# Two sequence mixers in scans of 1024 tokens instead of 512, with the other batch's PSUM banks, and a new order on every queue

## The reference

```python
# RWKV mixer, per channel, along the tokens
xk, xv, xr = mix(x, shifted)                  # and k = xk Wk', v = xv Wv', r = sigmoid(xr Wr')
p  = max(pp, u + k);  e1 = exp(pp - p);  e2 = exp(u + k - p)
out = (e1 * aa + e2 * v) / (e1 * bb + e2)
p2 = max(w + pp, k);  e1b = exp(w + pp - p2);  e2b = exp(k - p2)
aa, bb, pp = e1b * aa + e2b * v,  e1b * bb + e2b,  p2
# retention mixer: 16 heads of width 8
q, k = rope(q), rope(k)
out = einsum((q k' * 8**-0.5) * gamma**(s - t) for s >= t, v)
x += silu(x Wg') * groupnorm(out) @ Wo'
```

## Time and profile before

| | us |
|---|---|
| median of three runs (727.64 to 732.35) | 732.11 |
| the profiled execution, its own time | 732.31 |
| its span, first to last instruction | 730.4 |
| PE busy | 597.5 (82%) |
| DVE busy | 414.8 (57%) |
| POOL busy | 377.7 (52%) |
| ACT busy | 351.5 (48%) |
| mean granted TensorE clock | 0.934 |

### The profile page before, as it was taken

How to read it: one execution, slowest core, us unless ns; L and a number is a source line. 1 busy time by engine, 2 the same in 40 slices (tenths; PEclk the granted TensorE clock), 3 DMA queues, 4 the chain that set the end, 5 groups by cost and what they waited for, 6 DMA issues and landing times.

```text
span 730.4 us, 13064 instructions
## 1 busy us (share of the span) xinstructions
PE 597.5 (82%) x4172; PEld 505.0 (69%) x4172; DVE 414.8 (57%) x1166; ACT 351.5 (48%) x669; POOL 377.7 (52%) x396
## 2 busy tenths in 40 slices
PE   3489969998289888798979887999668699987892
PEld 2379968677267777788979886666434269986792
DVE  5744227797859963635056023879998896342002
ACT  2345656773158455554766554331111124665461
POOL 0467877432376337766775777124000276367762
PEclk9999989999599999998999998999799799999996
DMA  8295124001213012242231231000201012114313
GB/s 335 73 337 70 38 68 92 30 27 48 77 48 41 22 51 73 82 74 43 75 115 38 53 111 50 10 16 25 58 0 29 14 48 45 51 38 120 73 48 105
DMA packets 45120, 50.20 MB, mean 69 GB/s; under 512 B 14456, under 2 KB 36344, under 8 KB 45056
## 3 DMA queue, kind: packets, MB, share of 16 engines
q0 software_dynamic: 11776, 24.14, 14.3%
q1 hardware_dynamic: 33280, 25.23, 10.9%
HBM read 32.04 MB, written 17.29 MB: 68 GB/s over the span
## 4 chain that ended last, share of the span: by engine, by line
PE 48%; POOL 17%; DVE 14%; issue 10%; DMA 7%; ACT 3%; SPq 0%; ACTq 0%; DVEq 0%; POOLq 0%
PE bank L598 12%; POOL xs L1041 10%; PE bank L578 10%; POOL tokens_out L1051 7%; PE bank L585 6%; PE bank L677 5%; DMA xs<-tokens_in,idx_in 5%; PE bank L705 4%; PE bank L524 2%; PE bank L559 2%; DVE zT L1184 1%; PE bank L504 1%; ACT mixer L761 1%; PE bank L514 1%; DVE mixer L1321 1%
## 5 line engine op out<-in xcount | busy, mean ns | idle before, releaser
L1051 POOL DMA_INDIRECT tokens_out<-ys,idx_out x184 | 190.2, 1034 | 172.8 <-ACT ys L872 126.9
L1041 POOL DMA_INDIRECT xs<-tokens_in,idx_in x184 | 179.4, 975 | 161.2 <-DVE owner L1200 84.6
L598 PE MATMUL bank<-w,hT 128*128 x1288 | 180.9, 284 | 15.7 <-ACT ys L872 10.2
L598 PEld LDWEIGHTS bank<-w,hT 128*128 128x128 f32 x1288 | 164.1, 196 | 32.9 <-issue 31.6
L804 ACT ACTIVATE w_up<-w 128x728 f32 (+1 forms) x184 | 130.7, 718 | 106.2 <-PE bank L578 63.0
L578 PE MATMUL bank<-xT_kept,w_up 128*128 128x128 f32 x1104 | 155.9, 292 | 4.4 <-DVE hT L1220 2.3
L578 PEld LDWEIGHTS bank<-xT_kept,w_up 128*128 128x128 f32 x1104 | 145.3, 206 | 12.4 <-issue 6.7
L1220 DVE TENSOR_TENSOR hT<-gate,bank 128x384 f32<-128x384 f32 x92 | 50.7, 551 | 101.4 <-PE bank L578 71.0
L1236 DVE SCALAR_TENSOR_TENSOR x<-yg,cw,x 128x128 f32<-128x128 f32 x128 | 37.2, 339 | 116.2 <-DMA yg<-tokens_out 116.1
L585 PE MATMUL bank<-xT_kept,w_up 128*128 128x128 f32 x736 | 98.7, 284 | 0.7 <-issue 0.7
L585 PEld LDWEIGHTS bank<-xT_kept,w_up 128*128 128x128 f32 x736 | 91.6, 197 | 7.9 <-issue 7.1
(11 more groups left out here) (167 smaller groups left out, 631.1 us busy)
## 6 DMA issues: line engine op xcount, KB each, us to landing
yg<-tokens_out SPq DMA_DIRECT2D x64, 128.0 KB, 2.5
w<-in_w SPq DMA_DIRECT2D x8, 536.0 KB, 8.5
w<-in_w SPq DMA_DIRECT2D x8, 512.0 KB, 9.3
xs<-tokens_in,idx_in POOLq DMA_INDIRECT x184, 2.8
tokens_out<-ys,idx_out POOLq DMA_INDIRECT x184, 2.3
tokens_in<-xn SPq DMA_DIRECT2D x8, 256.0 KB, 6.6
tokens_in<-xn SPq DMA_DIRECT2D x8, 254.0 KB, 2.6
out<-x SPq DMA_DIRECT2D x8, 128.0 KB
```

The costliest lines, as they stand in the source:

```text
L598: last = mm(y, hT[0:n_f, n % 2, c * P:(c + 1) * P], w_of(k, e, WD[k] + c * P, P, n_f), start=(c == 0), stop=(k == 0 and c == CH[k] - 1))
L1041: pool.indirect_dma_start(xs[:, j % RING, :], None, xn_dram[KIND[f]][b], tile_rows(idx_in, b, j))\
L1051: pool.indirect_dma_start(ys_dram[b], tile_rows(idx_out, b, j), ys[:, j % RING, :], None)\
```

## The change

1. **RWKV** works on all 1024 tokens at once: k fills both banks of its batch (`pair[b]`), v both banks of the other batch (`pair[1 - b]`); 14 operations of 1024 columns take the place of 28 of 512, the exponents are two ACT instructions of 2048 columns (state first, then output), and r comes after v. Reciprocal, gate and output stay in halves.
2. **Retention** makes q and k of both halves first, then both gates, then eight turns in which v_j fills both banks of the batch and VectorE's three operations have 1024 columns; the sums lie in the other batch's two banks. The 16 state copies and the memset go; `r_m` stays double, `r_S` and `r_kv` are single.
3. **Waits for the borrowed banks.** v of RWKV(b) waits for the other batch's route table ("out"), and v of RWKV(0) also for `fold`; retention's first sum waits for the other batch's route; norm(1,1), norm(3,0) and norm(4,1) wait until the borrower is done.
4. **Weight load.** The eight loads of `w1` are eight pieces instead of one.
5. **Turns.** All five strings are new. They are quoted here only for SP, POOL and VectorE.

```diff
 TURNS "sp":
-        "e b a d a2 b2 c5 a6 b4 c b2 a6 c b6 a4 b4 a2 b2 a4 d4 b4 e4",
+        "e d a3 b3 c13 a4 c a2 b6 a6 c b6 a4 b3 a2 b3 a4 d4 b4 e4",
 TURNS "pool":
-        "f b g e a d c a c12 e c11 e5 d4 e4 a e a e a e6 d5 b e5 d14 f23 c23 e18 d3 e2 d e3 d4 f2 d3 f2 d4 f2 d3 f2 "
-        "d5 f6 c8 f6 c f c f2 c2 g c4 e2 c4 e2 c2 e2 c e8 d3 e2 d3 e2 d2 e2 d e2 d2 e d3 f2 d f2 d3 f2 d2 f2 d2 f2 d "
-        "f13 c20 e2 c3 e16 d4 e2 d2 e2 d e d16 f23",
+        "a g d c e f b a b c10 e2 c3 e2 c e2 c e2 c5 e c3 e5 d e2 d3 e2 d2 e2 d e3 d9 a d7 a2 f23 c16 e2 c4 e2 c3 e16 "
+        "d3 e3 d20 f14 c8 f9 c15 e2 g e14 d2 e2 d3 e5 d16 f10 d2 f13 c20 e2 c3 e20 d2 e d14 f d4 f2 d3 f20",
 TURNS "dve", end:
-        "... a7 c15 f c10 b76 c10 b c5 b9 c b c2 b c b c2 b c b2 c b c3 b c3 b c3 b c11 b c b c2 b2 c b c b "
-        "c b c2 b c b2 c54 b10 c10",
+        "... a7 c15 f c10 b71 c10 b c5 b3 c2 b c3 b c3 b c3 b c b2 c54 b10 c10",
@@ PSUM
-        bank = [ctx.enter_context(nc.psum_tensor(f"bank{i}", [P, HALF], F32)) for i in range(8)]
+        bank = [ctx.enter_context(nc.psum_tensor(f"bank{i}", [P, HALF], F32))[:, :] for i in range(4)]
+        pair = [ctx.enter_context(nc.psum_tensor(f"pair{b}", [P, S], F32))[:, :] for b in range(NB)]
+        bank += [pair[b][:, i * HALF:(i + 1) * HALF] for b in range(NB) for i in range(NH)]
@@ SP
+                for e in range(E):
+                    load_w(1, e)
+                    yield
@@ PE norm
+                    if (f, b) == (4, 1):
+                        after(RE_ACT[0], 0, f"sq{NH - 1}")
+                    if (f, b) in ((1, 1), (3, 0)):
+                        after(RW_DVE[1 - b], 0, "n2")
@@ PE rwkv
+                for i in range(NH):
+                    yield
+                    if i == 0:
+                        after(RT_DVE[1 - b], b, "out")
+                        if b == 0:
+                            after(FOLD_ACT, 0, f"e{E - 1}")
+                    yield from project("v", i, 1, bank[CB[1 - b] + i])
@@ PE retention
-                    project(i, ret[:, T_V:T_V + P], 0, (RE_DVE, f"kv0_{i}"))
...
+                for i in range(NH):
+                    yield
+                    project(i, ret[:, T_V:T_V + P], i, (RE_DVE, "kv0"))
+                for j in range(DH):
+                    if j + 1 < DH:
+                        for i in range(NH):
                             yield
-                            project(i, ret[:, T_V + (j + 1) * P:T_V + (j + 2) * P], 0, (RE_DVE, f"kv{j + 1}_{i}"))
+                            project(i, ret[:, T_V + (j + 1) * P:T_V + (j + 2) * P], i, (RE_DVE, f"kv{j + 1}"))
+                    for i in range(NH):
                         yield
+                        if j == 0 and i == 0:
+                            after(RT_DVE[1 - b], SUB[(3, 5)[b]], "out")
+                        after(RE_DVE[b], 0, f"m{j}")
+                        mm(bank[CB[1 - b] + i][:], ret[:, T_OUT + j * P:T_OUT + (j + 1) * P],
+                           r_m[:, j % 2, i * HALF:(i + 1) * HALF], start=(j == 0), stop=(j == DH - 1)).then_inc(RE_PE[b].sem, 1)
@@ DVE rwkv (exponents; the sums likewise)
+                after(RW_PE[b], 0, f"k{NH - 1}")
+                step(V.tensor_tensor_scan(pp1, w.to_broadcast([P, S]), k, rw_pp[:, 0:1], ALU.add, ALU.max))
@@ DVE retention
+                for j in range(DH):
+                    m = r_m[:, j % 2, :]
+                    yield
+                    after(RE_PE[b], 0, f"v{j}_{NH - 1}")
+                    done(f"S{j - 1}" if j else "k1")
+                    step(V.tensor_tensor(r_kv, k, pair[b], ALU.mult))
+                    yield
+                    done(f"kv{j}")
+                    step(V.tensor_tensor_scan(r_S, gamma[:, 0:1].to_broadcast([P, S]), r_kv, 0.0, ALU.mult, ALU.add))
+                    yield
+                    done(f"S{j}")
+                    if j >= 2:
+                        after(RE_PE[b], 0, f"o{j - 2}_{NH - 1}")
+                    step(V.tensor_tensor(m, q, r_S, ALU.mult))
```

More of the change, by code:

```diff
@@ L896, in gate_half @@
                     run(zT[:, b, i * HALF:(i + 1) * HALF], bank[CB[b] + i][:], ACT.Tanh, RW_ACT[b], scale=0.5)
[L898 to L900 removed]
+                for i, last in enumerate(("e2b", "e2")):
+                    yield
+                    after(RW_DVE[b], 0, last)
+                    ex = rw_ex[:, 2 * i:2 * i + 2, :].rearrange("p a b -> p (a b)")
                     run(ex, ex, ACT.Exp, RW_EXPS[b])
[L903 to L905 removed]
                 for i in range(NH):
@@ L916, in retention @@
             def retention(b):
+                parts = [slice(i * HALF, (i + 1) * HALF) for i in range(NH)]
                 for i in range(NH):
-                    part = slice(i * HALF, (i + 1) * HALF)
                     yield
@@ L1299, in rwkv_sums @@
+                num, den = e1b, e2b
+                v = pair[1 - b]
+                aa0, aa1 = rw_aa[:, 0:S], rw_aa[:, 1:1 + S]
+                bb0, bb1 = rw_bb[:, 0:S], rw_bb[:, 1:1 + S]
+                after(RW_EXPS[b], 0, "exp_state")
+                after(RW_DVE[b], 0, "e2")
+                step(V.tensor_tensor_scan(bb1, e1b, e2b, rw_bb[:, 0:1], ALU.mult, ALU.add))
+                yield
+                after(RW_PE[b], 0, f"v{NH - 1}")
                 step(V.tensor_tensor(rw_t, e2b, v, ALU.mult))
-                after(RW_DVE[b], 0, f"kv{i}")
@@ L1317, in rwkv_out @@
                 step = rwkv_step(b)
-                wkv, den = (rw_ex[:, i, a, :] for a in range(2))
-                after(RW_DVE[b], 0, f"den{i}")
+                wkv, den = (rw_ex[:, a, i * HALF:(i + 1) * HALF] for a in range(2))
+                after(RW_DVE[b], 0, "num")
                 step(V.reciprocal(den, den))
@@ L1330, in rwkv @@
             def rwkv(b):
-                for i in range(NH):
-                    yield
-                    yield from rwkv_exponents(b, i)
-                for i in range(NH):
-                    yield
-                    yield from rwkv_sums(b, i)
+                yield
+                yield from rwkv_exponents(b)
+                yield
+                yield from rwkv_sums(b)
                 for i in range(NH):
```

188 lines of the change are left out of this document (74 added, 114 removed), and 53 rows, old and new, of the table TURNS.

## The result

The changed kernel takes **700.2 us** (median of four runs, 697.82 to 701.56) against 731.6 for the kernel before: ratio 0.958, 95% interval 0.954 to 0.962. Five more runs of it, beside nine of the kernel before on another occasion, gave 698.85 against 731.8, ratio 0.956 (0.953 to 0.958). The profiled execution took 700.94, its span 699.0.

What follows compares the result with a forecast made beforehand. TensorE mostly bounds the kernel, with passes drying up twice while VectorE works; retention(0), retention(1), route(5,1) and pass (5,1) set the end. Terms -1 - 9 - 7 - 3 = -20 gave 712.3 us, range 702 to 727.

Steps and rivals of the forecast that it cites:

- Before retention(0): Middle passes up to retention's first operation: two ups and two downs fewer ahead on TensorE; -3 us, bounds +4 and -7.
- Start: Up to route(2,0): earlier last scatters of (0,0) remove TensorE's 5.53 us wait; -7 us, bounds 0 and -10.
- Wide operations: Merged VectorE operations of 1024 columns: product 1.221, scan 2.41, retention turn 4.86 us; 4.5 us saved per retention.
- Retention(0) and route(5,0): First retention's last product ends at 507.6 instead of 514.84, the following route's `idx` comes at 558 instead of 578.4.
- TensorE stays at its upper clock: During variance, Newton and norm of route(5,0), pieces of (3,1) keep TensorE at full clock; no separate time given.
- retention(1): Second retention, all turns behind route(5,0): last product ends at 604.6 against 606.34 before; stage forecast +18.7 us.
- Route(5,1): Route after the second retention: ends at 647, one us earlier; stage +0.6, whole chain term -1, bounds -6 and +5.
- Last pass: Pass (5,1): eight pieces less on TensorE, earlier scatters, against a 4 us hole; -9 us, bounds 0 and -14.
- A: Rival: only one of start and tail gains, the other is given back; 719 to 721 or 722 us, chance 0.17.
- B: Rival: nothing is won, since narrow halves overlapped and wide ones don't; 730 us, chance 0.10.
- C: Rival: slower, TensorE at its lower clock sets retention's turns; 752 us for ten turns, 740 for seven; chance 0.07.
- D: Rival: more is won, terms near their good bounds, -6, -14, -7 and -6; 699 us, chance 0.06.

Runs made afterwards that it cites:

- experiment 2: Kernel before with GpSimd's new order at the start and partly in the middle: 747.34 us, ratio 1.020; start alone, slow chip: 854.65, ratio 1.000.
- experiment 3: Changed kernel with retention's wide VectorE operations cut in two of 512 columns: 702.27 us, ratio 0.959; slow chip 848.42, ratio 0.980.
- experiment 6: Changed kernel with four TensorE pieces of (5,0) moved behind route(5,1)'s last table product: 705.75 us, ratio 0.965; slow chip 843.09, ratio 0.976.
- 7: Changed kernel with route(5,1)'s pieces, ScalarE copies and four gathers of (5,1) moved earlier on three queues: 845.86 us on a slow chip, ratio 0.981.

## Why the prediction was right or wrong

**Before retention(0): the step that failed.** "I take -3, bounds +4 and -7": measured -21.9, and -25.2 in the repeat. The step counted four pieces of TensorE (3.7 us) and said of the rest that the middle passes were "reordered without a reason I can price". That rest, put at nothing, is where the gain was. The -21.9 splits at the first gather and the last scatter of (3,0):

- From `te` of (2,0) to that gather 4.9 were gained.
- From the gather to the scatter it is 11.1. The kernel before has 66 gathers and scatters there in 90.4 us, 83.8 at 1.27 each: GpSimd was all but full, and what stood ahead of that scatter was on the chain. The changed kernel has 60 in 79.3 us. By count that is 6 x 1.27 = 7.6.
- From the scatter to retention(0) it took 29.0 and takes 23.2, 5.8 less, and VectorE's wait there fell from 11.23 to 6.37. This is the part that the step looked at.

What could have warned of it is TensorE's idle time in the last three stages, 24.0, and GpSimd without slack in the last; a bound of -7 had no such row behind it. The idle time isn't a strict bound either: of the gain in these three stages 12.3 is idle time and 9.1 is work moved behind retention(0).

**Whose order it was.** Not one queue's, as far as the runs show. GpSimd's old list of the middle in the changed kernel costs 24 us, as much as the term. The part of its new list that was put into the kernel before gains nothing and loses 16. Both runs show the same mechanism, TensorE waiting for gathers and GpSimd for ScalarE's copies of TensorE's products, each behind something that the other's list put later. The term belongs to lists that fit each other; TensorE's, ScalarE's and VectorE's lists alone weren't tried on a chip of 732 us. Width isn't it: retention's lies behind this stage, and all of it is worth 2 to 3.5 us. RWKV's has no part in it that shows on the slow chips; on a chip of 732 us that wasn't tested, nor were the borrowed banks.

On the slow chips the gain isn't there. From `te` of (2,0) to retention(0) the kernel with the old order (experiment 2, the start alone) takes 313.2 us, those with the new one (experiments 3, 6, 7) 315.6 to 321.3, one execution each on three chips. Its last part is shorter there as well, 56.1 from `te` of (3,1) against 67.5, but the part before it, from `te` of (3,0), takes 93.3 to 94.6 against 78.6. So the gain of the term was seen on chips of 732 us alone.

**Start, -7: right in size, not in cause.** The wait of 5.53 near 100 is gone, as the step said. But it is gone too in the kernel of experiment 2, from 80 to 115, and there GpSimd's order alone gave 1.2 us at `te` of (2,0) and, on a slow chip, nothing at the end: that wait wasn't what the chain hung on. RWKV's width, priced at 0 by "14 merged operations save 2.1, but its first scan needs both halves of k", was worth 2 to 5 us at that `te` on two slow chips. The rest is put down to the other lists, which isn't shown. That the term came out at -7.0 is luck.

**Wide operations.** The product was put at 1.221 and is 1.216 to 1.224, the scan at 2.41 and is 2.298, the turn at 4.86 and is 4.72. The slope of 2.21 ns per column, taken from 64 and 512 columns, was too steep: from 512 to 1024 it is 1.98. A cut product costs 0.06 more than a wide one (1.28, 1.29 against 1.22), the scan 0.25. The Trainium skill (Perfetto Trace Analysis, Optimizing Scalar/DVE Operations) puts an access overhead of about 60 ns on SBUF operations: by that the product in SBUF agrees, with 66 ns. Its 125 ns on PSUM does not show: L1401, one of whose two inputs lies in PSUM, saves 64. The same section says that the profiled latency of an instruction is longer than the time the engine is busy, because its end overlaps with the next instruction; the 1.28 for two durations of 0.68 bears that out.

**Retention(0) and route(5,0)** went by the working, -7.3 and -12.1 against -7.2 and -13.2, and so did retention(1), +17.9 against +18.7. The first gather of (5,0) came 48 us earlier, 30 forecast; the 18 more are the failed term. "TensorE stays at its upper clock" was wrong: from 490 to 530 the granted clock was 0.74. VectorE was busy there for 33.19 of 40 us, and the stage missed its term by 1.1; what of that is the clock wasn't measured.

**Route(5,1), +5.0 against +0.6.** Between retention(1)'s last sum and the table TensorE does 16 ups and 16 downs, before 14 and 15: three pieces more. The step counted two of them and then set them aside because "the table also waits for VectorE's own 6 us". TensorE was busy for 45.35 of the 46.0 us up to that `te`, VectorE waited 11.27 for the logits. The three pieces, at 0.92 each, are 2.8 of the 4.4 missed; the other 1.6 are open.

**Last pass, -5.9 against -9.** The hole was named ("about 4 us") and is 4.11, with the up products behind it at twice their time, at a granted clock of 0.53 from 627 to 634:

```profile
622.49 1.15 PE L599 MATMUL bank<-w,hT 128*128 x8 [0.52 <-ACT hT L839]
...
627.80 0.45 PE L560 MATMUL bank<-const,xs 128*128 128x128 f32 x1 [4.11 <-DMA xs<-tokens_in,idx_in]
...
632.00 2.08 PE L586 MATMUL bank<-xT_kept,w_up 128*128 128x128 f32 x8 [1.07 <-ACT xT_kept L828]
```

The waits for ring places did go. These two misses, 4.4 and 3.1, hid 7.5 of the 18.9 of the failed term: by that alone the time would have been 693.

The prediction's first reading of the page is in part wrong: TensorE's digits are 9 in the slices 26 to 28 and 33, and lower only from 29 to 32. No term hangs on it.

Of the rivals, A and B fell with the time, C with turns of 4.72 at a clock of 1.00 from 530 to 570. D had the time, 699, but for a wrong reason: it wanted -6, -14, -7 and -6, and got +3.5, -5.9, -7.0 and -21.9. Only the middle reached and passed its good bound.

## What to carry to other kernels

Lists written out for several in-order engines are one object: price them by following one tile through all queues, and expect that an edit of one list alone can lose, whichever way it goes: three did here, by 24, 16 and 6 us. Count a DMA-issuing engine's time as instructions times spacing, not as busy share: 42.4 of 55.5 was full. Where a stage can't be priced piece by piece, don't bound it tightly: the idle time of its busiest engines is a first measure, plus the work that the new order moves out of it (12.3 and 9.1 here). That is learnt from this one case and wasn't tried on another. And when ratios come from two sorts of chips, ask for the same stage on both before a gain is called one of the change.

## What was not expected of the hardware

Two VectorE operations in a row take less than their durations add up to: 1.28 us for two of 0.68. When the second needs the first's result it is different: the two halves of a scan, 1.254 each, take 2.54 (experiment 3). So durations add up along a dependence, and spacing, 0.60 here, is what independent halves pay.

The same kernel took 732 us on some chips and 853 to 864 on others. In the kernel of experiment 2 with the start alone, the nearest to it with a trace from there, VectorE's products and scans of 512 columns and more took the same within 2 ns; the granted TensorE clock was 0.87 against 0.93, TensorE's busy time 644.5 against 597.5 us and its idle time 207 against 133, with 43.5 us of waits (3.4 before) for which the profile names no releaser. The cause is open, and whatever was measured there says little of an order that was tuned on the other chips: from retention(0)'s first operation to retention(1)'s variance, cutting retention's operations cost 4.5 us here (161.6 against 157.1) and 11.1 there (170.1 against 159.0 in experiment 6).
